# Row norms begun in the stage ahead of them, and half of a gather added by VectorE

## The chip, the cores and the metric

The kernel runs on one NeuronCore of a Trainium2 chip. The metric is the device time of one execution in microseconds (us), the median of the runs. TensorE (PE) multiplies and transposes into PSUM; VectorE (DVE), ScalarE (ACT) and GpSimd (POOL) work on SBUF and PSUM; SyncE and GpSimd start DMA transfers. Each engine runs its own program in order and meets the others by semaphores.

## What is computed

A residual stream `x` of 2 x 1024 tokens with 256 features passes four layers. Each layer norms the rows, applies an attention (or what stands for one), adds, norms again, applies a feed-forward part, and adds:

```python
def _layernorm(x, axis=-1, eps=1e-05):
    m = jnp.mean(x, axis=axis, keepdims=True)
    v = jnp.var(x, axis=axis, keepdims=True)
    return (x - m) / jnp.sqrt(v + eps)
...
    x = x + jnp.tanh(g_xattn[0]) * _L0_xattn_ref(_layernorm(x), ctx_1024, ...)
    x = x + jnp.tanh(g_ffn[0]) * _L0_ffn_ref(_layernorm(x), ...)
    x = x + jnp.tanh(g_xattn[1]) * _L1_xattn_ref(_layernorm(x), ctx_1024, ...)
    x = x + jnp.tanh(g_ffn[1]) * _L1_ffn_ref(_layernorm(x), ...)
    x = x + jnp.tanh(g_xattn[2]) * _L2_xattn_ref(_layernorm(x), ctx_1024, ...)
    x = x + jnp.tanh(g_ffn[2]) * _L2_ffn_ref(_layernorm(x), ...)
    x = x + jnp.tanh(g_xattn[3]) * _L3_xattn_ref(_layernorm(x), ctx_1024, ctx_1024)
    x = x + jnp.tanh(g_ffn[3]) * _L3_ffn_ref(_layernorm(x), ...)
```

The `..._ref` parts that matter here: `_L0_ffn_ref` sends each token to one of eight experts; `_L1_xattn_ref` is a cross attention to 154 context tokens with a second layernorm of its own (gain and shift) and an output gate; `_L1_ffn_ref` sends each token to 4 of 16 experts, with two shared ones; `_L2_xattn_ref` is a linear attention; `_L2_ffn_ref` is two layers of local attention (window 128), each with a feed-forward part; `_L3_xattn_ref` multiplies by the context with a gelu between, and `_L3_ffn_ref` is a feed-forward part with weights and activations quantised to 4 bits.

## The kernel before

The 2048 tokens are T = 16 tiles of 128 rows, in G = 4 groups of four tiles (GT = 4, GN = 512 tokens). `x_tok`, the stream with tokens on partitions, stays in SBUF throughout. Each stage is a block of per-engine programs, run in the order in which they are written; all engines meet at a barrier between blocks. PSUM is used as eight banks of 128 x 512 values.

A row norm is a block of its own, `layer_norm` (L107). What can be had of it earlier is already had in the stage before: `RowStats.take` (L93) makes the statistics of each row (BN_STATS L96, BN_AGGR L99, by tile) as soon as its last add is done. `layer_norm` then has one chain: variance plus epsilon on VectorE (L144, or L142 where a second norm follows the first at once, `again`), the square root on ScalarE (L174), the inverse and minus mean times inverse on VectorE (L147, L149), then the 16 tiles, 13 on VectorE (L152) and three on ScalarE (L170), into `xn`. TensorE transposes each tile twice (L163) into eight banks of four, and ScalarE copies each bank to `xT`, features on partitions (L189, or L191 with gain and shift). With `keep` the tiles stay as they are and nothing is transposed (before the local attention, where eight tiles are ScalarE's). `root_table` (L104) loads ScalarE's table for the square root at the end of the stage before.

The square root and the activations of the feed-forward parts need different tables, so going from one to the other takes an ACT_TABLE_LOAD.

`feed_forward` (L214) serves the routed part and the local ones. For each group of 512 tokens it goes through units `u`: TensorE makes the hidden products, ScalarE the activation (L356 in the routed part), VectorE the gated product `hidden` (L429, L440), TensorE the output product; weights are split in two parts (upper and rest) beside that, on ScalarE (`weights_upper`, L341) and GpSimd. At the end of a group VectorE adds to x (`take`, L399 to L403) and takes statistics. The place where one group ends and the next begins is called a boundary below.

The stage ahead of the cross attention (L1716 to L1773) returns the expert outputs to their tokens: 16 indirect DMAs started by GpSimd (L1720), each 128 rows of 256 values, added in flight to `x_tok`; beside it VectorE makes remainders of weights (L211), copies the context's values out of PSUM (L1736) with their tails (L1741), and takes the statistics of each group when its four transfers have landed. GpSimd then makes the remainder of `wq` and `gated_bias` (L1725). Earlier, in the expert stage, L680 scatters 16 such tiles without an add. The name `oT` stands for attention outputs with features on partitions, `sd`, `rstd` and `minus_mean_rstd` for the root, its inverse and minus mean times it, one column for a tile.

## Time and profile before

| | |
|---|---|
| median of 3 runs | 2498.22 us (2495.98 to 2506.04) |
| the profiled execution | 2497.99 us, its span 2495.7 us |
| TensorE (matmul) busy | 2052.7 us, 82% |
| VectorE busy | 1759.9 us, 71% |
| ScalarE busy | 1327.8 us, 53% |
| GpSimd busy | 1045.6 us, 42% |
| mean granted clock | 0.905 |

All times in the rows below are microseconds from the start of the span, unless a column says ns. In a row of the timeline the first number is the start, the second the length (of a whole run of equal instructions where `x13` stands at the end), then engine, line, operation, output and inputs; the square brackets hold the idle time of the engine ahead of it and what ended that. PEclk is the granted clock of TensorE as a share of full speed: 1.00 is its upper level, 2.4 GHz.

### The profile page before, as it was taken

Reading aid. Unit: us, or ns where it says so; the run is one execution under the profiler, and the core shown is the slowest. Engines: PE = TensorE matmul, PEld = TensorE weight load, DVE = VectorE, ACT = ScalarE, POOL = GpSimd, SP = SyncE. Lnnn points to the kernel's source line nnn. Section 1 sums busy time; section 2 is a strip of 40 time slices with the busy share of each in tenths; the row PEclk is TensorE's granted clock in tenths of the full one; section 3 lists DMA queues with packets and bytes.
Section 4 is the critical chain, followed back from the end, with each engine's and each line's share of the span. In section 5 each row is a group of like instructions: output and inputs, shape, how many; then the busy total and the mean of one; then the engine's idle time right before and its main releaser. Section 6 shows DMA issues by size and latency. Waiting matters only on the chain. (4 is left out here: it accounts for less than half of the span.)

```text
span 2495.7 us, 41249 instructions
## 1 busy us (share of the span) xinstructions
PE 2052.7 (82%) x14744; PEld 1486.0 (60%) x14744; DVE 1759.9 (71%) x3778; ACT 1327.8 (53%) x3064; POOL 1045.6 (42%) x1053
## 2 busy tenths in 40 slices
PE   6899999966589997799997879886998886985254
PEld 5444444456556665688886668675877775764122
DVE  6899999855655554776765676766666675668896
ACT  4488888834354443333332247473436564323797
POOL 1333233115543431455553654543535452422554
PEclk9899999988799998899998989998998988987586
DMA  4244344154300001100002000002000001000000
GB/s 110 33 55 50 48 54 54 23 217 126 57 1 1 1 1 81 51 1 1 1 1 87 1 1 2 1 2 95 1 1 1 1 1 38 1 35 25 0 1 34
DMA packets 29257, 80.81 MB, mean 32 GB/s; under 512 B 6016, under 2 KB 20096, under 8 KB 27392
## 3 DMA queue, kind: packets, MB, share of 16 engines
q0 software_dynamic: 11136, 22.38, 7.2%
q1 hardware_dynamic: 17920, 55.80, 6.5%
q8 instruction: 120, 1.97, 0.3%
q14 instruction: 81, 0.66, 0.1%
...
## 5 line engine op out<-in xcount | busy, mean ns | idle before, releaser
L3028 ACT ACTIVATE probs<-psum 128x512 f32<-128x512 f32 (+1 forms) x640 | 344.0, 601 | 91.7 <-PE psum L2952 76.4
L3070 DVE TENSOR_REDUCE max_parts<-psum 128x1 f32<-128x512 f32 x512 | 320.1, 685 | 26.3 <-PE psum L2890 20.5
L199 PE MATMUL psum<-x_upper,weights_upper 128*128 128x512 f32 (+2 forms) x556 | 220.8, 397 | 27.5 <-POOL weights_rest L211 12.9
L211 POOL TENSOR_TENSOR weights_rest<-L1f,weights_upper 128x256 fp32r<-128x256 f32 x216 | 179.6, 858 | 147.9 <-ACT weights_upper L341 147.9
L2952 PE MATMUL psum<-q_stack,k_stack 50*128 50x512 f32 (+1 forms) x640 | 235.4, 453 | 0.2 <-ACT probs L3028 0.2
L199 PE MATMUL psum<-x_rest,weights_upper 128*128 128x512 f32 (+2 forms) x556 | 217.4, 391 | 0.0
L199 PE MATMUL psum<-x_upper,weights_rest 128*128 128x512 f32 (+2 forms) x556 | 216.3, 389 | 0.0
L2890 PE MATMUL psum<-k_stack,q_stack 48*128 48x512 f32 x512 | 192.6, 465 | 12.5 <-ACT probs L3028 7.8
L2962 PE MATMUL psum<-probs,v_tok 128*17 128x256 f32 x2560 | 194.7, 386 | 0.2 <-ACT probs L3028 0.2
L199 PE MATMUL psum<-weights_upper,hidden_upper 128*128 128x256 f32 (+1 forms) x572 | 178.2, 312 | 5.2 <-DVE hidden_rest L211 2.7
L2526 POOL TENSOR_TENSOR probs<-probs,row_sum 128x1024 f32<-128x1024 f32 x64 | 121.0, 1894 | 138.5 <-DVE row_sum L2545 138.5
L211 POOL TENSOR_TENSOR weights_rest<-L2f,weights_upper 128x256 fp32r<-128x256 f32 (+1 forms) x144 | 104.6, 755 | 163.1 <-ACT weights_upper L341 163.1
L199 PE MATMUL psum<-weights_upper,hidden_rest 128*128 128x256 f32 (+1 forms) x572 | 163.2, 285 | 0.0
L199 PE MATMUL psum<-weights_rest,hidden_upper 128*128 128x256 f32 (+1 forms) x572 | 163.0, 285 | 0.0
L2890 PEld LDWEIGHTS psum<-k_stack,q_stack 48*128 48x128 f32 x512 | 79.9, 189 | 124.2 <-DVE max_parts L3070 72.4
L2494 ACT ACTIVATE probs<-probs,row_least 128x256 f32<-128x256 f32 x256 | 126.9, 498 | 40.4 <-DVE row_least L2539 40.4
L2653 POOL DMA_DIRECT2D q_stack<-q_parts x56 | 30.5, 544 | 264.2 <-PE psum L2952 264.2
L199 PEld LDWEIGHTS psum<-x_upper,weights_upper 128*128 128x128 f32 (+1 forms) x556 | 105.9, 190 | 51.9 <-issue 24.4
L1934 ACT ACTIVATE L1x<-psum,row_least 128x154 f32<-128x154 f32 x256 | 95.4, 399 | 76.5 <-DVE row_least L1989 76.5
L1971 POOL TENSOR_TENSOR L1x<-L1x,row_sum 128x512 f32<-128x512 f32 x64 | 67.7, 1058 | 160.5 <-DVE row_sum L1994 160.2
L211 DVE TENSOR_TENSOR hidden_rest<-hidden,hidden_upper 128x512 fp32r<-128x512 f32 (+1 forms) x143 | 129.2, 903 | 4.9
L2391 POOL TENSOR_TENSOR cos_part<-cos_part,sin_part 128x1024 f32<-128x1024 f32 x32 | 76.5, 2389 | 116.0 <-DVE sin_part L2358 116.0
...
## 6 DMA issues: line engine op xcount, KB each, us to landing
...
```

The source lines that it names most:

```text
L199: ins = pe.matmul(out, lhsT(a).bitcast(F32R), rhs(b).bitcast(F32R), start=start and n == 0, stop=stop and n == len(PASSES) - 1, skip_group ...
L211: return engine.tensor_tensor(dst.bitcast(F32R), src, up_part, ALU.subtract)
L1934: ins = act.activation(ex[:, n % NE, h, :], net.ps[:, SLOT + 2 * s + e, a * SC:(a + 1) * SC], ACT.Exp, bias=mn[:, s, e, a:a + 1], scale=-1 ...
L1971: pool.tensor_tensor(main, ex[:, n % NE, :, 0:P], spread(sm[:, n % NE, :], P), ALU.mult)
L2391: pool.tensor_tensor(cp, cp, s_part[:, t % NSP].rearrange("p a n -> p (a n)"), ALU.add).then_inc(added, 1)
L2494: ins = act.activation(pb[:, n % NPB, h, :], pb[:, n % NPB, h, :], ACT.Exp, bias=mn[:, n % NPB, h:h + 1], scale=-1.0, accum_out=sm[:, n % ...
L2526: pool.tensor_tensor(pb[:, n % NPB], pb[:, n % NPB], spread(sm[:, n % NPB, :], 2 * P), ALU.mult)\
L2890: ins = pe.matmul(out, qs[s][r, a * P:(a + 1) * P].bitcast(F32R), ks[s][r, k * 512:(k + 1) * 512].bitcast(F32R), start=True, stop=True)
L2952: pe.matmul(net.ps[0:m, ST + n % NS, :], ks[s][r, k * P:k * P + m].bitcast(F32R), qs[s][r, :].bitcast(F32R), start=True, stop=True).then_i ...
L2962: ins = pe.matmul(net.ps[32 * j:32 * j + HD + 1, PVB, 0:256], vt[:, b, k, h, :], pb[:, n % NPB, j * 256:(j + 1) * 256], start=k == 0, stop ...
L3028: act.activation(pb[0:m, n % NPB, (1 - e) * 512:(2 - e) * 512], net.ps[0:m, ST + (2 * n + e) % NS, :], ACT.Exp, scale=HD ** -0.5)\
L3070: ins = v.tensor_reduce(mx3[:, u % 2, a + 4 * e, k:k + 1], src, AX.X, ALU.max)
```

## The change

Five of the eight norms are changed: those before the cross attention, the routed part, the linear attention, the local attention and layer 3.

A new class `NormAhead` holds the steps of `layer_norm` as separate calls: `spread` (variance plus epsilon), `root`, `invert` (the inverse, and minus mean times it), `vector` and `scalar` (the tiles). The preceding stage calls them for twelve of the sixteen tiles: after each group of four where the stage goes by groups (cross attention's norm, and those before the linear attention and layer 3, which follow a feed-forward part), or once for twelve. The tiles are written to a buffer `nT` (`norm_turned` in the rows), or to `y` where nothing is transposed first. `norm_end` takes the place of `layer_norm`: statistics and norm of the last four tiles, all 32 transposes, and the copies out of PSUM, seven banks by ScalarE and one by VectorE. The transposes go in place: the banks are copied back to `nT`, which takes the place of `xT`. Several buffers of other stages share its room.

In the feed-forward parts the root comes at `u == 2` of the next group, the inverse at `u == 2` of VectorE's program, and ScalarE's four tiles at `u == 3`. The order of ScalarE's program then has 12 more table loads (two at each of six boundaries).

In the stage with the gather the first eight transfers write plain rows to the upper half of `nT`, and VectorE adds them to `x_tok`, four tiles at a time (L1906 of the changed kernel); the last eight add in flight as before. The remainder of `wq` and `gated_bias` go from GpSimd to VectorE, the tails of the context's values from VectorE to ScalarE.

VectorE in the stage with the gather, from the first copies of the context's values on, before (`row_stats` and `mean_var` are the statistics, `values` and `tail_values` the context's):

```order
L1736 COPY values<-psum 128x512 x2
L211 TENSOR_TENSOR wo_rest<-L1x,wo_upper 128x2048
L96 BN_STATS row_stats<-x_tok 128x6 x4
L99 BN_AGGR mean_var<-row_stats 128x2 x4
L1741 COPY tail_values<-psum 32x2x64 x8
L96 BN_STATS row_stats<-x_tok 128x6 x4
L99 BN_AGGR mean_var<-row_stats 128x2 x4
L1736 COPY values<-psum 128x512 x2
L96 BN_STATS row_stats<-x_tok 128x6 x4
L99 BN_AGGR mean_var<-row_stats 128x2 x4
L1741 COPY tail_values<-psum 32x2x64 x8
L96 BN_STATS row_stats<-x_tok 128x6 x4
```

and now (`rows_var_eps`, `rows_sd`, `rows_rstd` are columns of four tiles):

```order
L1900 COPY values<-psum 128x512 x2
L1906 TENSOR_TENSOR x_tok<-x_tok,norm_turned 128x1024
L98 BN_STATS row_stats<-x_tok 128x6 x4
L101 BN_AGGR mean_var<-row_stats 128x2 x4
L209 TENSOR_SCALAR rows_var_eps<-mean_var 128x4
L340 TENSOR_TENSOR wo_rest<-L1x,wo_upper 128x2048
L224 RECIPROCAL rows_rstd<-rows_sd 128x4
L226 SCALAR_TENSOR_TENSOR rows_minus_mean_rstd<-mean_var,rows_rstd 128x4
L1900 COPY values<-psum 128x512 x2
L340 TENSOR_TENSOR wq_rest<-L1x,wq_upper 128x2048
L1939 TENSOR_SCALAR gated_bias<-L1x,cross_factor 128x256
L1906 TENSOR_TENSOR x_tok<-x_tok,norm_turned 128x1024
```

The tails are gone, an add of 1024 elements precedes the statistics of a group, and the remainder of `wq` and the bias stand between the first and second group; the inverse for a group waits here for ScalarE's root.

ScalarE where the cross attention ends and the routed part begins, before (`oT_upper` is the attention's output, `warm` a dummy that loads the table):

```order
L1941 CAST oT_upper<-psum 128x512 x4
L104 ACT_TABLE_LOAD
L104 ACTIVATE warm<-warm 128x1
L1776 UNCONDITIONAL_BRANCH
L167 UNCONDITIONAL_BRANCH
L174 ACTIVATE sd<-var_eps 128x16
L170 ACTIVATE xn<-x_tok,minus_mean_rstd,rstd 128x256 x3
L189 COPY xT<-psum 128x512 x8
```

and now:

```order
L106 ACT_TABLE_LOAD
L106 ACTIVATE warm<-warm 128x1
L2112 CAST oT_upper<-psum 128x512 x2
L218 ACTIVATE rows_sd<-rows_var_eps 128x12
L243 ACTIVATE norm_turned<-x_tok,rows_minus_mean_rstd,rows_rstd 128x2x128 x8
L1947 UNCONDITIONAL_BRANCH
L299 UNCONDITIONAL_BRANCH
L305 COPY norm_turned<-psum 128x512 x2
L218 ACTIVATE rows_sd<-rows_var_eps 128x4
L305 COPY norm_turned<-psum 128x512
L243 ACTIVATE norm_turned<-x_tok,rows_minus_mean_rstd,rows_rstd 128x2x128
L305 COPY norm_turned<-psum 128x512 x4
```

The root for twelve tiles, and eight of those tiles, now precede the end of the stage (the first UNCONDITIONAL_BRANCH), and the root of the last four stands among the copies of the transposed banks.

ScalarE at a boundary of the routed part, before (`activated` is the gate's activation, `weights_upper` the upper parts of the weights of a unit):

```order
L341 CAST weights_upper<-L1f 128x256 x3
L356 ACTIVATE activated<-psum 128x512
L341 CAST weights_upper<-L1f 128x256 x3
L356 ACTIVATE activated<-psum 128x512
L341 CAST weights_upper<-L1f 128x256 x3
```

and now:

```order
L471 CAST weights_upper<-L1f 128x256 x3
L218 ACT_TABLE_LOAD
L218 ACTIVATE rows_sd<-rows_var_eps 128x4
L486 ACT_TABLE_LOAD
L486 ACTIVATE activated<-psum 128x512
L471 CAST weights_upper<-L1f 128x256 x3
L243 ACTIVATE norm_turned<-x_tok,rows_minus_mean_rstd,rows_rstd 128x2x128 x4
L486 ACTIVATE activated<-psum 128x512
```

The root with a table load on either side stands ahead of one activation, and the four tiles ahead of the next.

The diff, cut:

```diff
+class NormAhead:
+
+
+    def __init__(self, net, ctx, src, place, again=False):
+        self.net, self.src, self.place, self.again = net, src, place, again
...
+    def spread(self, v, lo, hi):
+
+        r = self.net.rows
+        if self.again:
+            ins = v.tensor_scalar(r.ve[:, lo:hi], r.mv[:, lo:hi, 1], 1.0 + EPS, EPS * EPS, ALU.mult, ALU.add)
+        else:
+            ins = v.tensor_scalar(r.ve[:, lo:hi], r.mv[:, lo:hi, 1], EPS, None, ALU.add)
+        ins.then_inc(self.var_ready, 1)
+
+    def root(self, act, part, lo, hi):
+
+        r = self.net.rows
+        act.wait_ge(self.var_ready, part + 1)
+        act.activation(r.sd[:, lo:hi], r.ve[:, lo:hi], ACT.Sqrt).then_inc(self.sd_ready, 1)
+
+    def invert(self, v, part, lo, hi):
+
+        r = self.net.rows
+        v.wait_ge(self.sd_ready, part + 1)
+        v.reciprocal(r.rs[:, lo:hi], r.sd[:, lo:hi]).then_inc(self.rs_ready, 1)
+        v.wait_ge(self.rs_ready, part + 1)
+        v.scalar_tensor_tensor(r.nb[:, lo:hi], r.mv[:, lo:hi, 0], -1.0, r.rs[:, lo:hi], ALU.mult, ALU.mult)\
+            .then_inc(self.rows_ready, 1)
+
+    def vector(self, v, tiles):
+
+        r = self.net.rows
+        for t in tiles:
+            dst, own = self.place(t)
+            v.tensor_scalar(dst, own(self.src), r.mv[:, t, 0:1], r.rs[:, t:t + 1], ALU.subtract, ALU.mult)\
+                .then_inc(self.normed, 1)
+
+    def scalar(self, act, part, tiles):
+
+        r = self.net.rows
+        act.wait_ge(self.rows_ready, part + 1)
+        for t in tiles:
+            dst, own = self.place(t)
+            act.activation(dst, own(self.src), ACT.Identity, bias=r.nb[:, t:t + 1], scale=r.rs[:, t:t + 1])\
+                .then_inc(self.normed, 1)
+
...
+def norm_end(net, ahead, parts, turns=None, xT=None, gain=None, shift=None, after=None):
+
+    nc = net.nc
+    LO = T - GT
...
+            step = Steps(v, vec)
+            net.rows.take(v, step, ahead.src, range(LO, T))
+            step.settle()
+            ahead.spread(v, LO, T)
+            ahead.invert(v, parts, LO, T)
+            ahead.vector(v, OWN)
+            if turns:
+                if after is not None:
+                    v.wait_ge(after.landed, 16)
+                v.wait_ge(early, BY_VECTOR + 1)
+                c = BY_VECTOR % C
+                if gain is None:
+                    v.tensor_copy(out(BY_VECTOR), net.ps[:, BY_VECTOR, :])
+                else:
+                    v.tensor_scalar(out(BY_VECTOR), net.ps[:, BY_VECTOR, :], gain[:, c:c + 1], shift[:, c:c + 1],
+                                    ALU.mult, ALU.add)
+
...
+            def _(pe):
+                for n in range(G * C):
+                    g, c = divmod(n, C)
+                    if n == BY_VECTOR:
+                        pe.wait_ge(ahead.normed, T)
+                    for t in range(g * GT, (g + 1) * GT):
+                        ins = pe.transpose(net.ps[:, n, t % GT * P:(t % GT + 1) * P], turns(t, c), net.ident[:])
+                    ins.then_inc(early, 1)
...
+                take(0)
+                take(1)
+            ahead.root(act, parts, LO, T)
+            if turns:
+                take(2)
+            ahead.scalar(act, parts, OTHER)
+            if turns:
+                for n in range(3, G * C):
+                    if n != BY_VECTOR:
+                        take(n)
...
+                if ahead is not None and g >= 1 and u == 2:
+                    ahead.root(act, g - 1, (g - 1) * GT, g * GT)
+                if ahead is not None and g >= 1 and u == 3:
+                    ahead.scalar(act, g - 1, range((g - 1) * GT, g * GT))
...
+                if ahead is not None and g == G - 1:
+                    return
                 net.rows.take(v, step, y if then is None else x, range(g * GT, (g + 1) * GT))
+                if ahead is not None:
+                    step.settle()
+                    ahead.spread(v, g * GT, (g + 1) * GT)
...
+                if ahead is not None and g >= 1 and u == 2:
+                    ahead.invert(v, g - 1, (g - 1) * GT, g * GT)
...
+            ahead.root(act, 0, 0, T - GT)
+            ahead.scalar(act, 0, range(GT, T - GT))
...
+            ahead.spread(v, 0, T - GT)
+            ahead.invert(v, 0, 0, T - GT)
+            ahead.vector(v, range(GT))
             for k in (PAIRS - 2, PAIRS - 1):
                 add_y(k)
-                statistics(k)
...
+        beside_x = lambda t, n: nT[:, t // GT, 2 * GN + t % GT * D:2 * GN + (t % GT + n) * D]
...
+                def tail_value(n):
+                    b, tail, half = v_items[n]
+                    act.wait_ge(v_made, n + 1)
+                    src = net.ps[:, 4 + n % 4, :]
+                    for i in range(4):
+                        r = slice(SEG * i, SEG * i + SEG)
+                        mine = lambda ap: ap.rearrange("p (q i) d -> p i q d", i=4)[:, i]
+                        ins = act.copy(mine(vz[r, b, half * 8:half * 8 + 8, :]),
+                                       mine(src[r].rearrange("p (h d) -> p h d", d=64)))
+                    ins.then_inc(tail_taken, 1)
...
+                act.wait_ge(cleared, 1)
+                tail_value(2)
+                tail_value(3)
+                for g in range(G - 1):
+                    ahead.root(act, g, g * GT, (g + 1) * GT)
+                    if g == 0:
+                        tail_value(6)
+                        tail_value(7)
+                    ahead.scalar(act, g, range(g * GT, (g + 1) * GT))
...
-                    pool.indirect_dma_start(x[:, t, :], None, slots_y, bass.IndirectOffsetOnAxis(slots[:, n:n + 1], 0),
-                                            compute_op=ALU.add)\
-                        .then_inc(gathered[t // GT], 16)
-                pool.wait_ge(wq_upper, 1)
-                rest(pool, wq[1][:], w("wq"), wq[0][:])
-                pool.tensor_scalar(gbo[:], w("bo"), factor, None, ALU.mult)
+                    at = bass.IndirectOffsetOnAxis(slots[:, n:n + 1], 0)
+                    if t < 2 * GT:
+                        pool.indirect_dma_start(beside_x(t, 1), None, slots_y, at).then_inc(gathered[t // GT], 16)
+                    else:
+                        pool.indirect_dma_start(x[:, t, :], None, slots_y, at, compute_op=ALU.add)\
+                            .then_inc(gathered[t // GT], 16)
...
+
+                def rows_of(g):
                     v.wait_ge(gathered[g], 16 * GT)
+                    if g < 2:
+                        xs = x[:, g * GT:(g + 1) * GT, :].rearrange("p t d -> p (t d)")
+                        step(v.tensor_tensor(xs, xs, beside_x(g * GT, GT), ALU.add))
+                        step.settle()
                     net.rows.take(v, step, x, range(g * GT, (g + 1) * GT))
+                    step.settle()
+                    ahead.spread(v, g * GT, (g + 1) * GT)
...
-                for n in range(len(v_items)):
-                    value(n)
-                    if n == 1:
-                        v.wait_ge(wo_upper, 1)
-                        rest(v, wo[1][:], w("wo"), wo[0][:])
-                    if n % 2:
-                        add(n // 2)
-
-        layer_norm(net, x, xT, again=True, gain=w("gain"), shift=w("shift"))
+                value(0)
+                value(1)
+                rows_of(0)
+                v.wait_ge(wo_upper, 1)
+                rest(v, wo[1][:], w("wo"), wo[0][:])
+                ahead.invert(v, 0, 0, GT)
+                value(4)
+                value(5)
+                v.wait_ge(wq_upper, 1)
+                rest(v, wq[1][:], w("wq"), wq[0][:])
+                v.tensor_scalar(gbo[:], w("bo"), factor, None, ALU.mult)
+                rows_of(1)
+                ahead.invert(v, 1, GT, 2 * GT)
+                rows_of(2)
+                ahead.invert(v, 2, 2 * GT, 3 * GT)
+                v.wait_ge(gathered[G - 1], 16 * GT)
...
+        norm_end(net, ahead, G - 1, lambda t, c: nT[:, c, t * P:(t + 1) * P], nT, gain=w("gain"), shift=w("shift"))
...
-                net.rows.root_table(act)
+                then.root(act, 0, 0, T - GT)
+                then.scalar(act, 0, range(GT, T - GT))
...
+                        if u == U + 1 and d == 0:
+                            then.invert(v, 0, 0, T - GT)
+                            then.vector(v, range(GT))
...
+                        if u == U and d == 1:
+                            step.settle()
+                            then.spread(v, 0, T - GT)
...
-                for k in range(6, 8):
-                    rows_of(k)
...
-            layer_norm(net, x, xT)
+            norm_end(net, routed, 1, turns, nT)
...
+                    norm_end(net, linear_in, G - 1, turns, nT)
...
+                norm_end(net, local_in, 1)
...
-                layer_norm(net, x, None, keep=y)
...
+                norm_end(net, last_in, G - 1, lambda t, c: y[:, t, c * P:(c + 1) * P], nT)
```

## Rows read from the trace of the kernel before

**Rows 1.** The cores: span and mean granted TensorE clock.
```profile
core 0: 2495.7 us, clock 0.905
```

**Rows 2.** Timeline, cross attention to routed layer: start, duration, engine, line, operation, idle.
```profile
981.94 0.75 DVE L2023 SCALAR_TENSOR_TENSOR x_tok<-psum,cross_factor,x_tok 128x512 f32<-128x512 f32 x1 [5.01 <-PE psum L1625]
984.30 0.25 DVE L99 BATCH_NORM_AGGREGATE mean_var<-row_stats 128x2 f32<-128x6 f32 x2
987.26 0.17 DVE L144 TENSOR_SCALAR var_eps<-mean_var 128x16 f32<-128x16 f32 x1 [2.71 <-PEq L3247]
988.10 4.28 DVE L152 TENSOR_SCALAR xn<-x_tok,mean_var,rstd 128x256 f32<-128x256 f32 x13
989.53 5.92 PE L163 MATMUL psum<-const,xn 128*128 128x128 f32 x32 [7.63 <-DVE xn L152]
990.68 0.58 ACT L189 COPY xT<-psum 128x512 f32<-128x512 f32 x1 [0.88 <-PE psum L163]
...
996.48 1.92 PE L477 MATMUL psum<-xT,const 128*32 128x512 f32 x16 [1.02 <-PEq L114]
```

**Rows 3.** Timeline, the norms before the linear attention and before layer 3.
```profile
1343.16 0.18 DVE L144 TENSOR_SCALAR var_eps<-mean_var 128x16 f32<-128x16 f32 x1 [3.04 <-PEq L3360]
1349.14 2.55 ACT L189 COPY xT<-psum 128x512 f32<-128x512 f32 x5 [0.27 <-PE psum L163]
...
2240.93 0.17 DVE L144 TENSOR_SCALAR var_eps<-mean_var 128x16 f32<-128x16 f32 x1 [2.86 <-PEq L3412]
2246.90 2.54 ACT L189 COPY xT<-psum 128x512 f32<-128x512 f32 x5 [0.27 <-PE psum L163]
```

**Rows 4.** Timeline of the gather and its norm; instructions of two lines (ns min/median/max).
```profile
657.52 2.28 DVE L211 TENSOR_TENSOR wo_rest<-L1x,wo_upper 128x2048 fp32r<-128x2048 f32 x1
...
676.48 1.41 DVE L96 BATCH_NORM_STATS2 row_stats<-x_tok 128x6 f32<-128x256 f32 x4 [3.36 <-DMA x_tok<-slots_y,slots]
678.10 1.52 POOL L1725 TENSOR_SCALAR gated_bias<-L1x,cross_factor 128x256 f32<-128x256 f32 x1
681.27 0.17 DVE L142 TENSOR_SCALAR var_eps<-mean_var 128x16 f32<-128x16 f32 x1 [2.98 <-PEq L1647]
684.70 5.93 ACT L191 ACTIVATE xT<-psum,L1x 128x512 f32<-128x512 f32 x8 [0.88 <-PE psum L163]
...
L680 POOL DMA_INDIRECT slots_x<-xn,slots x16: 965/969/1105, 552.5 to 571.7; - x16
...
L1720 POOL DMA_INDIRECT x_tok<-slots_y,slots x16: 1537/1546/3564, 642.2 to 672.6; - x16
```

**Rows 5.** Timeline, a group boundary of the routed layer; a table load.
```profile
1107.47 0.60 ACT L356 ACTIVATE activated<-psum 128x512 f32<-128x512 f32 x1 [1.95 <-PE psum L293]
1109.21 0.47 PE L199 MATMUL psum<-x_upper,weights_upper 128*128 128x512 f32 x1 [0.34 <-DVE hidden L440]
1112.46 0.60 ACT L356 ACTIVATE activated<-psum 128x512 f32<-128x512 f32 x1 [2.54 <-PE psum L293]
...
1333.17 1.28 ACT L104 ACT_TABLE_LOAD   x1
```

**Rows 6.** Second local feed-forward; windows: length, PE, PEld, DVE, ACT, POOL, PEclk.
```profile
2158.41 0.47 PE L199 MATMUL psum<-x_upper,weights_upper 128*128 128x512 f32 x1 [1.61 <-DVE hidden L429]
...
2150.00:2179.80 29.80, 28.19 (x156) 22.88 (x154) 18.71 (x34) 9.98 (x24) 12.37 (x18) 1.00 0.00 1
2179.80:2211.30 31.50, 30.52 (x153) 24.73 (x153) 18.37 (x34) 9.98 (x24) 13.01 (x18) 0.89 0.00 1
```

**Rows 7.** Timeline, the end of the linear attention and the norm behind it.
```profile
1428.76 0.59 ACT L1058 COPY oT<-psum 128x512 f32<-128x512 f32 x1 [2.91 <-PE psum L983]
1434.99 0.17 DVE L144 TENSOR_SCALAR var_eps<-mean_var 128x16 f32<-128x16 f32 x1 [1.74 <-PEq L81]
1435.94 4.04 ACT L170 ACTIVATE y_tok<-x_tok,minus_mean_rstd,rstd 128x256 f32<-128x256 f32 x8 [0.53 <-DVE minus_mean_rstd L149]
1440.29 3.64 PE L2261 MATMUL psum<-const,y_tok 128*128 128x128 f32 x16 [8.90 <-PEq L114]
```

141 lines of the change are left out of this document (87 added, 54 removed).

## The prediction, made before the change was run

> **What bounds the kernel now.** I began with spans and clock: one core, 2495.7 us [rows 1]; the profiled execution took 2497.99 us, 0.2 below the median of the runs (2498.22), so a sum made on the trace stands for the median within a microsecond. The stages run one after another and no single engine bounds all of them, so I read next the timeline where one stage ends and the next begins (a seam). There TensorE, busy on both sides, waits for a row norm. At the seam into the routed layer the last add into x starts at 981.94 and lasts 0.75, statistics follow until 984.55, the norm's first instruction comes at 987.26, TensorE transposes from 989.53 on (5.92 for 32), and the next stage's first matmul is at 996.48 [rows 2]: 13.8 us from the end of the add. The reader is to see that there the norm itself is the chain: VectorE, TensorE and ScalarE follow each other by tile. The seams before the linear attention and before layer 3 have the same form, 8.53 us (1343.16 to 1351.69) and 8.51 us (2240.93 to 2249.44) [rows 3]. Before the cross attention the timeline shows GpSimd as the latest: the gather, then two operations until 679.62, then a norm from 681.27 to 690.63 [rows 4].
>
> **The piece that all four seams share (`norm_end`).** Twelve of sixteen tiles are now normalised ahead, so TensorE may transpose at once. Three chains run in it. TensorE: 32 transposes, 5.92 [rows 2], then the copy of the last bank, 0.58 and 0.2 of latency: 6.7. VectorE: statistics of the last four tiles 1.9 (984.55 less 982.69), the chain of four short steps 0.84 (987.26 to 988.10), three tiles at 0.33 (4.28 over 13): 3.7 [rows 2], and the last eight transposes wait for it, which TensorE doesn't reach before 4.4 (24 of 32 of 5.92). ScalarE: first copy 1.15 after TensorE starts [rows 2], seven at 0.51 (2.55 over 5) [rows 3], a square root 0.2 and a tile 0.5: 5.5. TensorE is last, 6.6 to 6.7; I take 6.6. For the cross attention with gain and shift a copy takes 0.74 (5.93 over 8) [rows 4], so ScalarE is last: 1.15 + 5.2 + 0.7 = 7.1.
>
> **Part by part.** *Routed layer.* Add to norm was 4.57 with 1.86 of statistics in it; now 2.71. Then 6.6 and 0.3 to the next stage against 9.22 (987.26 to 996.48) [rows 2]. Saved: 13.8 - 9.6 = 4.2. The root, the inverse and the other twelve tiles lie under the 11 us in which TensorE makes the last output projection; if that cover were gone ScalarE's eight tiles alone would cost 4.0 [rows 7]. *Linear attention.* 8.53 + 1.86 - 6.6 = 3.8. *Layer 3.* The same with 8.51: 3.8. Their weights are fetched 1.9 earlier as well, so no landing becomes late.
>
> *Local attention.* Here nothing turns, and the gain vanishes into a new wait. VectorE now stands at `invert` until ScalarE has copied the last oT (1428.76 + 0.59) and taken the root: 1429.6. Behind it on VectorE are four tiles (1.4) and the last two adds into x, which end near 1432.9. ScalarE has eight tiles, 4.04 [rows 7], from 1430.1 to 1434.2, and ends the stage. Then 0.3 to `norm_end`, 1.9 + 0.8 + 1.1 in it and 1.75 for the barrier: 1440.1 against 1440.29 [rows 7]. The barrier's 1.75 is the idle time before 1434.99. Saved: 0.2, between -0.8 and 1.0.
>
> *The stage with the gather.* Before, the last transfer lands and statistics start at 676.48; GpSimd ends at 679.62 and the norm starts at 681.27 [rows 4]. The remainder of wq and the bias leave GpSimd, so its tail goes. What is late next is a chain through VectorE and ScalarE. From 657.5 VectorE has: add 1.15 (half of the 2.28 for 2048 elements), statistics and variance 2.2, wo 2.28, inverse 0.5, two value copies 1.3, wq 2.28, bias 0.4, add and statistics 3.3, root and inverse 0.8, statistics 2.2: 673.9. Then root, inverse 0.8 and ScalarE's four tiles 2.1: 676.8, +0.3 for the barrier: 677.1. The tail values moved to ScalarE lie before this: it had nothing to do from the end of its table load to the norm.
> The transfers must also be there. One issue with add in flight takes 1.55, with up to 3.56 beside VectorE's wo remainder; the plain scatter takes 0.97 [rows 4]. The trace has no plain gather, so its issue lies between 0.97 and 1.55. I take 0.97, as the scatter is the same instruction without the add. Eight issues less 0.58 are 4.6 saved; the added VectorE work may hold issues up by some 1.6 (wo held one up by 2.0). The last landing goes from 676.4 to 673.5, before 676.8, and is hidden. With 1.55 it would be 678.1. Dearer than 1.55 I exclude, the same 128 rows without the add; below nothing there is no price. Saved: 690.63 - (677.1 + 7.1) = 6.4; 4.9 with the dear issue.
>
> *Added inside the stages.* Two feed-forwards (routed, second local) get, at three group boundaries each, on VectorE a settle and a variance (0.3) and an inverse (0.5), on ScalarE two table loads of 1.28, a root 0.2 and four tiles 2.1. The first sits straight ahead of the product that TensorE waits for at the boundary (0.34 in the routed layer [rows 5], 1.61 in the local one [rows 6]): 0.3 each, 1.8 in all. The inverse comes where VectorE has caught up: nothing. ScalarE: its activations at the boundary start at 1107.47 and 1112.46, 4.99 apart, with 1.6 of its own work between [rows 5]; root and loads (2.8) fit into the 3.4 left, the tiles (2.1) into the next. If that cover were gone, see below. The cross attention pays 0.3 for the same variance ahead of its last remainder.
>
> **Sum.** 6.4 + 4.2 + 3.8 + 3.8 + 0.2 = 18.4 saved, 2.1 paid: 16.3. From 2498.2 that is 2481.9; I say 2482.
>
> **Rivals.** *The gather stays the bound* (plain issue 1.55, VectorE's new operations delay issues). For: 3.56 in place of 1.55 beside one VectorE operation. Against: the scatter's 0.97. Then that seam saves 4.9 or, with 2 us more of delay, 3: total 13 to 15, 2484.
> *The clock falls at more boundaries.* The second local feed-forward's group 2179.80 to 2211.30 had a clock of 0.89, and TensorE was busy for 30.52 in it against 28.19 for the same work in the group before (1.00) [rows 6], each after a pause of about 1.6. If longer pauses do this at all six boundaries, five new ones cost 2.0 each: 6 saved, 2492. Against: two of three such pauses did nothing to it.
> *ScalarE's table changes are dearer.* In the trace the load lasts 1.28, and nothing stands between it and the operations about it [rows 5]. If each change cost 1.4 more, boundaries would have 5.5 in 3.4 of room, 2.1 late at six places: 3.7 saved, 2494.5. The Trainium skill ("ScalarE: Activation LUTs", What ACT_TABLE_LOAD costs) says just this, a load of about 1283 ns and a drain of about 1380 ns, 2.66 us for every change. The load agrees with the trace, the drain isn't seen there.
> *Slower.* ScalarE is in order: if the three activations behind each root have no room, the 4.9 us of loads, root and tiles and the 0.8 on VectorE reach TensorE at six places, 34 us against 18.4: 2514. It decides once a boundary costs more than 3.1 us. Against: TensorE has two more units' products in hand before it needs an activation, and ScalarE idles 1.95 and 2.54 before them [rows 5].
> *It doesn't shorten the seams* (transposes at a low clock and the copies make `norm_end` as long as the old norm less its statistics): 4 x 1.9 + 4 saved, less 2: 2489.
>
> **How the numbers follow.** Forecast 0.58; gather 0.15; clock 0.13; tables 0.03; seams not shorter 0.07; slower 0.04. A measurement of this kernel tells about 0.5% (12.5 us) from no change, so faster means below 2485.7: the forecast and most of the gather's rival, 0.73; within 0.5%: 0.23; slower 0.04. The forecast's own spread (norm_end 5.8 at a full clock or 7.3, boundaries 0 to 0.8 each, gather seam 4.9 to 7) is 2476 to 2486. To leave no more than 0.2 out, the range reaches to the clock's case: 2475 to 2492.
>
> **What would show it.** Transposes start with the block, and `norm_end` lasts 6.6 (7.1 in the cross attention); the stage with the gather ends with ScalarE's tiles, not with GpSimd; plain gathers take 0.97 to issue; TensorE waits 0.6 and 1.9 at the boundaries; the next stage starts at the local attention as before. Wrong would be: a ScalarE activation that TensorE waits for right behind a root, a plain gather as dear as the adding one, low clock in more groups, or a wait for weights behind a shorter norm.

## The result and the profile after

The changed kernel took 2479.31 us (median of four runs, 2475.72 to 2483.35), 0.992 of before (95% interval 0.9903 to 0.9938), 19.5 us less than the 2498.80 of the four runs of before that stood beside it. It was measured again beside the experiments, six runs each: 2474.77 (ratio 0.9905, 0.9881 to 0.9929) and 2473.85 (0.9893, 0.9877 to 0.9908). Over the 16 runs the median is 2475.2; over 41 runs of before it is 2499.0. The forecast was 2482 with a range of 2475 to 2492.

The profiled execution is the slowest of the first four (2483.35), so its span is only 14.3 us shorter than that of [rows 1]:

```profile
core 0: 2481.4 us, clock 0.909
```

I cut both executions at the same points of the program. Each line below is one window of the changed kernel: its length, the busy time of PE, PEld, DVE, ACT and POOL with counts, the granted clock, the DMA share and GB/s. The windows are, in order:

- up to the first product of the keys;
- from there to the first query product (the stage with the gather and its norm);
- from the end of the cross attention's last add to the routed part's first product;
- three groups of the routed part, from add to add;
- from its last add to the linear attention's first product;
- the linear attention, up to the first product of the local one;
- from the second local feed-forward's first add to layer 3's first product.

```profile
0.00:650.10 650.10, 563.50 (x4976) 300.86 (x4977) 516.77 (x1005) 437.08 (x877) 186.19 (x290) 0.93 0.41 76
650.10:691.89 41.79, 26.09 (x128) 22.66 (x128) 29.92 (x70) 28.47 (x63) 23.41 (x16) 0.82 0.26 47
981.42:989.85 8.43, 3.90 (x32) 3.49 (x33) 3.96 (x16) 4.39 (x10) 0.04 (x1) 1.00 0.82 321
1096.05:1329.09 233.04, 231.31 (x1318) 195.43 (x1316) 162.90 (x254) 97.89 (x225) 127.03 (x150) 1.00 0.00 1
1329.09:1340.49 11.40, 5.36 (x32) 5.18 (x33) 5.36 (x17) 4.43 (x10) 0.04 (x1) 0.85 0.66 255
1340.49:1428.52 88.03, 70.99 (x304) 52.68 (x305) 55.88 (x132) 27.60 (x47) 52.43 (x42) 0.89 0.07 29
2142.61:2242.02 99.41, 84.62 (x464) 69.61 (x465) 63.00 (x128) 47.32 (x97) 31.91 (x45) 0.95 0.10 38
```

The lengths beside those of before and of the two later profiles of the same kernel, in us:

| stretch | before | after | again | again_2 |
|---|---|---|---|---|
| first key to first query product | 48.65 | 41.79 | 42.30 | 42.28 |
| cross attention's last add to routed part | 13.79 | 8.43 | 8.43 | 9.98 |
| three groups of the routed part | 232.35 | 233.04 | 232.99 | 233.00 |
| last routed add to linear attention | 15.51 | 11.40 | 11.42 | 11.40 |
| linear attention to local attention | 87.93 | 88.03 | 88.04 | 88.04 |
| first add of the second local part to layer 3 | 102.92 | 99.41 | 99.44 | 100.85 |
| sum of these, against before | | -19.05 | -18.53 | -15.60 |
| all the rest of the span, against before | | +4.75 | -5.47 | +10.60 |

The reader is to see two things. The stretches that the change touches agree from profile to profile, and give 15.6 to 19 us. The rest does not agree: it moves by 16 us between profiles of one kernel. Up to the first key product the code is the same as before, and it took 644.60 us before and 650.10, 643.58 and 654.90 after.

One part of this rest lies right behind a touched stretch, and the prediction has no term for it. These are the first 12 us of the local attention, before, in the changed kernel and in its third profile (again_2):

```profile
1440.29:1452.29 12.00, 10.51 (x46) 8.98 (x47) 5.65 (x11) 4.18 (x7) 0.00 (x0) 0.82 0.00 0
1428.52:1440.52 12.00, 10.51 (x34) 8.65 (x35) 3.17 (x7) 3.37 (x5) 0.00 (x0) 0.53 0.00 1
1438.66:1450.66 12.00, 10.50 (x41) 8.83 (x41) 4.32 (x8) 4.17 (x7) 0.00 (x0) 0.67 0.00 1
```

The granted clock was 0.82 before and 0.53 and 0.67 in these two; in the same 10.5 us TensorE has 46 matmuls before, 34 and 41 after. From the first product to ScalarE's eighth `squares` of that stage it took 42.70 us before, and 45.34, 45.34 and 44.04 in the three profiles of the changed kernel, so 1.3 to 2.6 us are lost there. Other kernels with the same norm ahead of it took 42.69 to 45.37, so these runs don't show that the shorter norm is the cause.

At the seam into the routed part, against [rows 2], transposes start with the block, beside the statistics, and the old chain VectorE, TensorE, ScalarE is gone:

```profile
980.67 0.75 DVE L2197 SCALAR_TENSOR_TENSOR x_tok<-psum,cross_factor,x_tok 128x512 f32<-128x512 f32 x1 [5.01 <-PE psum L1769]
984.14 2.81 PE L296 MATMUL psum<-const,norm_turned 128*128 128x128 f32 x24 [3.52 <-PEq L3423]
984.81 1.07 ACT L305 COPY norm_turned<-psum 128x512 f32<-128x512 f32 x2 [11.64 <-PE psum L296]
...
986.73 1.05 DVE L234 TENSOR_SCALAR norm_turned<-x_tok,mean_var,rows_rstd 128x256 f32<-128x256 f32 x3
987.84 1.09 PE L296 MATMUL psum<-const,norm_turned 128*128 128x128 f32 x8 [0.89 <-DVE norm_turned L234]
...
989.85 1.92 PE L618 MATMUL psum<-norm_turned,const 128*32 128x512 f32 x16 [0.92 <-PEq L263]
```

The short norm, up to the next stage's first product, takes 5.7 us (984.14 to 989.85), and 8.43 pass from the end of the add (980.67 + 0.75) to the next stage, where it was 13.8.

The stage with the gather, against [rows 4]:

```profile
673.29 0.34 DVE L1939 TENSOR_SCALAR gated_bias<-L1x,cross_factor 128x256 f32<-128x256 f32 x1
675.09 1.53 POOL L1890 DMA_INDIRECT x_tok<-slots_y,slots  x1 [0.30 <-issue]
680.12 2.07 ACT L243 ACTIVATE norm_turned<-x_tok,rows_minus_mean_rstd,rows_rstd 128x256 f32<-128x256 f32 x4 [0.44 <-DVE rows_minus_mean_rstd L226]
682.50 1.41 DVE L98 BATCH_NORM_STATS2 row_stats<-x_tok 128x6 f32<-128x256 f32 x4 [2.41 <-PEq L1792]
...
686.50 2.77 ACT L307 ACTIVATE norm_turned<-psum,L1x 128x512 f32<-128x512 f32 x4
...
L1888 POOL DMA_INDIRECT norm_turned<-slots_y,slots x8: 949/956/1957, 647.7 to 658.4; - x8
...
L1890 POOL DMA_INDIRECT x_tok<-slots_y,slots x8: 1531/1546/3643, 659.6 to 675.1; - x8
```

GpSimd ends at 676.6 and ScalarE's last tiles end the stage at 682.2, 32.1 us behind the first key product; the forecast had 32.5 (677.1 less 644.6). A plain transfer takes 0.95 us to issue, one that adds 1.55. The long ones have a neighbour on VectorE:

```profile
667.05 2.28 DVE L340 TENSOR_TENSOR wo_rest<-L1x,wo_upper 128x2048 fp32r<-128x2048 f32 x1
667.10 3.64 POOL L1890 DMA_INDIRECT x_tok<-slots_y,slots  x1 [0.30 <-issue]
671.05 1.53 POOL L1890 DMA_INDIRECT x_tok<-slots_y,slots  x1 [0.30 <-issue]
671.08 2.30 DVE L340 TENSOR_TENSOR wq_rest<-L1x,wq_upper 128x2048 fp32r<-128x2048 f32 x1
```

The issue that began 0.05 us behind the start of a remainder took 3.64; the one that began 0.03 ahead of the next remainder took 1.53, though the two ran side by side.

A boundary of the routed part, against [rows 5], and the one of the second local part, against [rows 6]:

```profile
1099.03 0.60 ACT L486 ACTIVATE activated<-psum 128x512 f32<-128x512 f32 x1 [1.95 <-PE psum L423]
1100.98 0.47 PE L328 MATMUL psum<-x_upper,weights_upper 128*128 128x512 f32 x1 [0.57 <-DVE hidden L579]
1101.49 1.28 ACT L218 ACT_TABLE_LOAD   x1
1102.79 0.21 ACT L218 ACTIVATE rows_sd<-rows_var_eps 128x4 f32<-128x4 f32 x1
1103.01 1.28 ACT L486 ACT_TABLE_LOAD   x1
1104.30 0.60 ACT L486 ACTIVATE activated<-psum 128x512 f32<-128x512 f32 x1
1106.61 2.08 ACT L243 ACTIVATE norm_turned<-x_tok,rows_minus_mean_rstd,rows_rstd 128x256 f32<-128x256 f32 x4
1108.66 0.60 ACT L486 ACTIVATE activated<-psum 128x512 f32<-128x512 f32 x1
...
2150.91 0.47 PE L328 MATMUL psum<-x_upper,weights_upper 128*128 128x512 f32 x1 [1.83 <-DVE hidden L568]
```

TensorE waits 0.57 and 1.83 us. The activation behind the root starts at 1104.30, 5.27 after the one before; their regular distance is 4.4 (1104.30 to 1108.66), so it is 0.9 late. TensorE has no second wait behind it.

### The profile page after: what moved, and what is told of

It reads as the page before. It is cut to its first block and busy times, and to the rows that moved or that the text cites. A ratio compares the mean times of both kernels' runs of the same rounds, so it can differ in the third digit from the quotient of the medians.

```text
span 2481.4 us, 41330 instructions
## 1 busy us (share of the span) xinstructions
PE 2054.0 (83%) x14744; PEld 1484.2 (60%) x14744; DVE 1747.8 (70%) x3765; ACT 1364.9 (55%) x3137; POOL 1038.5 (42%) x1051
```

## The experiments

Each starts from the changed kernel. Lengths of stretches come from one profile of each. I trust these over the whole times, since the whole also carries what the unchanged stages do. Four kernels have one run each, so their whole times prove little: 2490.52 us with more table changes, 2487.41 with late transposes, 2479.79 with the remainder of wq on GpSimd and 2491.36 with only the norm ahead.

### All transfers add in flight

```diff
-                    if t < 2 * GT:
+                    if t < 0:
                         pool.indirect_dma_start(beside_x(t, 1), None, slots_y, at)...
-                    if g < 2:
+                    if g < 0:
                         xs = x[:, g * GT:(g + 1) * GT, :].rearrange("p t d -> p (t d)")
```

> The changed kernel, but all sixteen transfers of the gather add in flight and VectorE adds nothing. My theory: the plain rows give GpSimd 0.6 us for each of eight transfers and cost VectorE 1.22 for each of two adds. In the profile of the changed kernel the stage ends with ScalarE's tiles (682.2), 0.4 us behind them the last transfer could land; with all in flight GpSimd ends some 4 us later and so is the last of the stage, while VectorE and ScalarE are 2.4 earlier. Expected: the stage (first key product to the first query product) takes 43 to 45 us in place of 41.8, that is 1 to 3 us more, and the whole 1 to 3 us more than the changed kernel. Rival 'the plain rows are what the gather stage gained': the stage goes back by 4 us or more, towards 48.7. Rival 'the plain rows bring nothing': it stays within 0.5 us or gets faster by the 2.4 of the adds.

Measured: first key to first query product 43.04 us, so the plain rows are worth 1.25 us against the first profile of the changed kernel and 0.75 against the other two. The last issue starts 28.5 us behind the first key product (25.0 in the changed kernel), and the stage now ends with it:

```profile
678.88 2.07 ACT L243 ACTIVATE norm_turned<-x_tok,rows_minus_mean_rstd,rows_rstd 128x256 f32<-128x256 f32 x4 [0.44 <-DVE rows_minus_mean_rstd L226]
679.78 1.55 POOL L1890 DMA_INDIRECT x_tok<-slots_y,slots  x1 [0.30 <-issue]
...
684.56 1.41 DVE L98 BATCH_NORM_STATS2 row_stats<-x_tok 128x6 f32<-128x256 f32 x4 [5.71 <-PEq L1792]
```

ScalarE's tiles end at 680.95, the last transfer has been issued at 681.33 and lands after that. The stage went as expected. The whole did not: 2492.84 us (six runs, 2486.46 to 2493.97), 13.5 more than the changed kernel's first result. I ran it again beside the changed kernel on one chip.

> The kernel with all sixteen transfers adding in flight once more, beside the changed kernel on one chip. On the first chip it took 2492.8 us, where its stage is only 1.25 us longer than the changed kernel's (43.04 against 41.79). Theory 'the 11 us beyond are the clock of that chip': here it takes 0 to 4 us more than the changed kernel. Rival 'transfers that add in flight slow later stages': it again takes 8 us or more beyond the changed kernel.

Measured: 2479.78 (ratio to before 0.9931, 0.991 to 0.9952) beside 2473.85 for the changed kernel; the stage took 43.10 us. So of the 12 us that the first run took beyond its stage some 5 are left. Both theories miss: I had given 0 to 4 for the one and 8 or more for the other. The unchanged part of its first profile was 13.5 us longer than before, of its second 2.5 us shorter. What makes it so stays open.

### The remainder of wq on GpSimd again

```diff
             def _(pool):
...
+                pool.wait_ge(wq_upper, 1)
+                rest(pool, wq[1][:], w("wq"), wq[0][:])
+                pool.tensor_scalar(gbo[:], w("bo"), factor, None, ALU.mult)
```

(and the same lines taken out of VectorE's program)

> The changed kernel with one move undone: the remainder of wq and the gated bias are GpSimd's again, behind its last transfer. My theory: the gather stage got shorter because its last chain ran through GpSimd (3.9 us for the two behind the last transfer in the trace before), not only because its transfers are cheaper. In the changed kernel GpSimd ends its last transfer at 676.6; with the two operations it ends near 680.5 to 682.5 (the add on VectorE holds it up), and VectorE is 2.6 us earlier, so ScalarE's tiles end near 679.6. Expected: the stage takes 41 to 43 us in place of 41.8, near to nothing either way, since the plain transfers have made room for them; together with the all-in-flight run this would say that either edit alone is enough and that the second adds little. Rival 'the move is what counted': the stage goes back by 3 us or more.

Measured: 45.00 us, 3.2 more than in the changed kernel's first profile and 2.7 more than in the one on the same chip (42.30). My expectation was wrong, and what came is the rival's 3 us, or a little less. The rows:

```profile
675.70 5.26 DVE L226 SCALAR_TENSOR_TENSOR rows_minus_mean_rstd<-mean_var,rows_rstd 128x4 f32<-128x4 f32 x1
675.86 5.08 POOL L340 TENSOR_TENSOR wq_rest<-L1x,wq_upper 128x2048 fp32r<-128x2048 f32 x1
...
680.88 1.39 DVE L98 BATCH_NORM_STATS2 row_stats<-x_tok 128x6 f32<-128x256 f32 x4
...
681.00 2.07 ACT L243 ACTIVATE norm_turned<-x_tok,rows_minus_mean_rstd,rows_rstd 128x256 f32<-128x256 f32 x4 [5.54 <-DVE rows_minus_mean_rstd L226]
...
683.60 2.07 ACT L243 ACTIVATE norm_turned<-x_tok,rows_minus_mean_rstd,rows_rstd 128x256 f32<-128x256 f32 x4 [0.44 <-DVE rows_minus_mean_rstd L226]
```

An operation on four columns, 0.16 us elsewhere in the same stage, took 5.26 us: it ended when GpSimd's operation of 5.08 us ended, and statistics and ScalarE's tiles stood behind it. GpSimd itself was done at 681.84; the stage ends with ScalarE's tiles at 685.67. I had reckoned the engines' work apart; here one holds up the other. The Trainium skill ("SBUF — State Buffer", Who interferes with whom) says that VectorE and GpSimd share a pair of SBUF ports and that the one that holds it blocks the other for its whole instruction; the 5.26 beside 5.08 agrees, though by the rows VectorE's operation began 0.16 us ahead of GpSimd's. In the same section the Trainium skill infers that a two-input VectorE operation doesn't hold up GpSimd's making of descriptors. The issue of an indirect transfer is held up all the same: an adding transfer took 3.56 us beside the 2048-element remainder, and 3.64 in the changed kernel, in place of 1.55. Both began while the remainder ran, and both ended 1.4 us behind its end. An indirect transfer also takes its row numbers from `slots`, a tile in SBUF, so these rows don't tell whether that read is held up or the descriptors are.

### Only the norm ahead

Both edits of the gather taken back together.

```diff
-                    if t < 2 * GT:
+                    if t < 0:
...
+                rest(pool, wq[1][:], w("wq"), wq[0][:])
```

> The changed kernel with both edits of the gather taken back: all transfers add in flight, and the remainder of wq and the gated bias are GpSimd's behind the last of them; the norm ahead stays. My theory: GpSimd is the last again, 30.0 + 5.1 + 0.9 us behind the first key product, as before the change (35.0), and only the shorter norm is left as a gain, 9.4 less 6.8 us. Expected: the stretch from first key product to first query product takes 46 to 47.5 us (48.65 before, 43.0 without the plain rows, 45.0 without the move). Rival 'the edits are worth the same alone and together': 41.8 + 1.25 + 3.2 = 46.2; rival 'the norm ahead gives the whole': below 44.

Measured: 46.50 us. In this stage the norm ahead saves 2.15 us (48.65 less 46.50). From there the plain rows bring 1.5 (to 45.00) or the move 3.4 (to 43.07, the mean of 43.04 and 43.10). Both bring 4.2 to 4.7, so the two edits nearly add up. They don't meet in one queue, though. Here GpSimd is the last of the stage: its `gated_bias` ends at 680.66 and the statistics behind the stage's end start at 682.31. With all transfers adding it is a transfer's landing, and with the remainder on GpSimd it is ScalarE, which waited for VectorE, which waited for GpSimd.

### The tail shared

```diff
-                    ahead.scalar(act, g, range(g * GT, (g + 1) * GT))
+                    ahead.scalar(act, g, range(g * GT, (g + 1) * GT - (2 if g == 2 else 0)))
+                    if g == 0:
+                        act.activation(gbo[:], w("bo"), ACT.Identity, scale=factor)
...
                 ahead.invert(v, 2, 2 * GT, 3 * GT)
+                ahead.vector(v, (3 * GT - 2, 3 * GT - 1))
```

> The changed kernel with its last chain in the gather stage shortened: the gated bias is ScalarE's (between its first and second group of tiles, where it waited 2.3 us), and of the third group's four tiles VectorE does two beside ScalarE's two. My theory: that stage now ends with VectorE's work and ScalarE's last four tiles (680.12 to 682.19); 0.34 us of VectorE's work and 1.0 of ScalarE's go. Expected: the stretch from first key to first query product takes 40.3 to 40.9 us in place of 41.8 (42.3 in its second profile). Rival 'a transfer is the last by then': it stays within 0.3 us.

Measured: 41.06 us, 0.7 to 1.2 less than the changed kernel's three profiles, a little short of what I expected. That the stage ends with VectorE and ScalarE is so. The whole took 2481.49 us (0.9917, 0.9896 to 0.9939), so a gain of the whole can't be shown: it drowns in what the unchanged stages do.

### The feed-forward parts without the norm ahead

```diff
-                         ahead=linear_in)
+                         ahead=None)
...
-                    norm_end(net, linear_in, G - 1, turns, nT)
+                    layer_norm(net, x, nT, keep=y)
```

(and the same for `last_in`)

> The changed kernel with the old row norm before the linear attention and before layer 3 (nothing of it in the two feed-forward parts ahead). My theory: these two seams give 4.1 and 3.5 us back and the six boundaries save about 0.25 us each, so 7.6 - 1.5 = 6 us more than the changed kernel; the wait of TensorE at a boundary goes back from 0.57 to 0.34 and from 1.83 to 1.6 us, and groups of the routed part from 79.69 to 79.44 us. Rival 'boundaries cost nothing by themselves, the difference of the two profiles is chance': groups stay at 79.7. Rival 'the seams gain only what the clock gives': each seam gives back under 2 us.

Measured: the two seams 15.65 and 19.89 us (11.40 and 16.29 in the changed kernel, 15.51 and 19.78 before), the three routed groups 232.36 (233.04, 232.35). Everything is back to within 0.2 us of before, and all else of the change stays. The touched stretches are 11.6 us shorter than before, and the whole is 11.5 shorter: 2487.51 beside 2498.99 (0.9955, 0.9941 to 0.9968). So on the medians the account by stretches closes here, though this kernel's own profile was, with 2496.90, among its slower runs and 10.8 us longer in the unchanged rest. A boundary costs 0.23 us (233.04 less 232.36, over three).

### More table changes at the boundaries

```diff
...
                     ahead.root(act, g - 1, (g - 1) * GT, g * GT)
+                    for _ in range(g - 1):
+                        for f in (func, ACT.Sqrt):
+                            net.spare = getattr(net, 'spare', 1) + 1
+                            act.activation(net.rows.warm[:, net.spare:net.spare + 1], net.rows.warm[:, 0:1], f)
```

> The changed kernel with more table changes of ScalarE at the boundaries of the routed and of the second local feed-forward part: none more at the first boundary, one pair (activation's table and back, 2 x 1.28 us and two dummies of 0.2, 3.0 us) behind the root at the second, two pairs (6.0 us) at the third. My theory: in the changed kernel the activation behind the root is 0.9 us later than its turn in the routed part and nobody waits for it, since TensorE has two units in hand; a unit of TensorE takes 4.4 us there. The first boundary stays at 79.7 us for its group; with 3.0 us more the activation is 3.9 late, within one unit, and TensorE waits under 1 us; with 6.0 us more it is 6.9 late and TensorE waits 1.5 to 4 us. In the local part the second boundary costs under 1 us and the third 1 to 4. Rival 'no room was left' (the price of the slower case): the second boundary already costs 3 us and the third 6. Rival 'ScalarE has room for all': neither moves by 0.3 us.

Measured: routed groups 79.68, 79.68 and 78.02 us (79.69, 79.64 and 73.71 in the changed kernel). So 3.0 us more of loads cost nothing, and 6.0 us cost 4.3. The new wait of TensorE at the third boundary:

```profile
1266.90 0.47 PE L328 MATMUL psum<-x_upper,weights_upper 128*128 128x512 f32 x1 [0.56 <-DVE hidden L583]
...
1278.42 0.47 PE L328 MATMUL psum<-x_upper,weights_upper 128*128 128x512 f32 x1 [2.49 <-DVE hidden L583]
```

The second of these rows is the 2.49 us that TensorE newly waits for a product whose activation was late. The other 1.8 us are the clock behind that wait. In the routed groups of the changed kernel it was 1.00 throughout; here, from the end of the wait on:

```profile
1278.42:1290.00 11.58, 11.57 (x55) 9.47 (x56) 9.21 (x13) 5.81 (x15) 7.46 (x9) 0.85 0.01 1
```

At 0.85 for 11.58 us about 1.7 are lost (my estimate, 0.15 of the window). In the local part the second boundary is unchanged and the third costs 1.9 (25.58 against 23.73). So the mechanism of the prediction's slower case exists, but ScalarE can be at least 3.0 us later than the change makes it before TensorE waits. The 3.1 us in that case are another quantity, what each boundary would have to cost TensorE to eat up the gain.

### Late transposes at one seam

```diff
-                    if n == BY_VECTOR:
+                    if n == (0 if late else BY_VECTOR):
                         pe.wait_ge(ahead.normed, T)
```

(ScalarE's root and tile ahead of its first copies, for this seam alone)

> The changed kernel with one seam altered, from cross attention to the routed part: TensorE begins its transposes only when all sixteen tiles are normed, and ScalarE takes the root and its tile before its first copy. TensorE's pause goes from 3.5 to about 7 us, as long as before the change (7.6). Two causes are told apart for the 1.2 us that this seam gained beyond the forecast, and the 1.8 us that the first group behind it gained. Theory 'clock': with the short pause the granted clock stayed at 1.00 through the seam (24 transposes in 2.81 us, 0.117 each) where it was 0.63 before; with the long pause it falls, 32 transposes take 5.5 to 6 us, and the first group of the routed part goes back from 106.2 to 107 or 108 us. The seam is then 3.4 + 2 to 3 longer. Rival 'the order': the transposes keep 0.117 each, only the wait is added (3.4 us), and the first group stays at 106.2.

Measured: the seam 13.75 us, before's 13.79, with the norm's twelve tiles still ahead. TensorE's pause is 7.21 us and its 32 transposes took 6.42:

```profile
985.36 6.42 PE L296 MATMUL psum<-const,norm_turned 128*128 128x128 f32 x32 [7.21 <-DVE norm_turned L234]
```

The three kernels beside it had a seam of 9.0, with a pause of 3.51 and transposes of 5.35, so 3.7 of the added 4.8 us are the wait and 1.1 the clock. What the seam gains is that TensorE works beside VectorE's statistics, not that tiles are made elsewhere: without that overlap nothing is left. (The old norm had an overlap of its own, transposes beside the making of tiles, which this kernel lacks as well.) That fits the prediction's account of three chains. On the clock this run looked like a proof. The first group behind the seam took 108.33 us, as 'clock' wanted. But all three kernels beside it took 108.33 to 108.35 with the short pause, so that part had nothing to do with the edit.

### TensorE kept busy

```diff
+def keep_busy(net, pe, bank, n):
+    for _ in range(n):
+        pe.transpose(net.ps[:, bank, 0:P], net.ident[:], net.ident[:])
...
+            if ahead is not None:
+                keep_busy(net, pe, GATE, 12)
```

(20 more in the short norm ahead of the local attention, 24 in the stage with the gather)

> The changed kernel with transposes of the identity added on TensorE where it only waits; their results are read by nobody: 12 at the end of the two feed-forward parts that precede a norm, 20 in the short norm before the local attention, and 24 in the stage of the gather, from the point where the second group's row columns are ready. My theory: after a shorter pause the granted clock is higher, and a part of the time at the seams is TensorE at the lower level (32 transposes took 5.36 us at a mean clock of 0.74 before the linear attention and 2.81 for 24 where the clock had stayed at 1.00; the first 10 us of the local attention had 0.50). Expected: the transposes before the linear attention and layer 3 take 3.9 to 4.7 us, the seams get 0.3 to 1 us shorter each (ScalarE's copies are next, 5.5), the local attention begins at a higher clock and gains 1 to 3 us; sum 2 to 5 us less than the changed kernel. Rival 'the clock after a pause does not hang on these pauses' (or the added work itself draws the clock down): no stretch changes by 0.3 us, or other stretches give it back.

Measured: 2475.89 us (0.9899, 0.9882 to 0.9915) beside 2474.77, no gain. At the seam before the linear attention the pause ahead of the transposes went from 4.80 to 3.49 us, and they took longer, 6.51 in place of 5.36:

```profile
1333.85 5.36 PE L296 MATMUL psum<-const,norm_turned 128*128 128x128 f32 x32 [4.80 <-PEq L3546]
```

and with the added transposes:

```profile
1335.32 6.51 PE L296 MATMUL psum<-const,norm_turned 128*128 128x128 f32 x32 [3.49 <-PEq L3560]
```

That seam became 1.1 us longer (12.56 against 11.42), and the linear attention behind it 1.5 (89.52 against 88.04 to the first local product). The local attention did get faster, 43.49 us to the eighth `squares` against 45.34, but other kernels of that chip without the added work had 44.00 and 42.73, so this gain is not shown either. 'The clock follows the pause' falls with this. At the seam into the routed part a pause of 3.5 us was followed by transposes of 3.90 us in five profiles, 5.35 in six and 6.34 in one. Four kernels of one chip had 3.90, and on another three of three had 5.35, which looked like a mark of the chip until the next run:

> The changed kernel on the chip of the three runs beside it. Two things are open. Its first and second measurement gave 19.5 and 23.9 us less than before, while the seven changed stretches of the profiles add up to 18.7; and on one chip the seam into the routed layer took 8.43 us in four kernels of four, on another 9.0 in three of three. Theory 'the rest is the clock of unchanged stages, and differs by chip': the seam takes 8.4 or 9.0 here in all kernels of this call alike, the changed stretches again add up to 18 to 19.5 us, and what the whole deviates from that goes with the mean granted clock. Rival 'a gain of the change that I have not found': the difference is 22 us or more at an equal sum of the stretches and with no difference in unchanged stages.

There the seam took 9.98 us in the changed kernel and 9.00, 8.99 and 8.99 in its three neighbours on the same chip. Neither theory of that run holds in full: the seam differs within one chip, and the difference to before was 27 us (2473.85 against 2500.82) where the stretches gave 15.6, though in a profile that was itself the slowest run of six (2492.64).

### The changed kernel again

> The changed kernel itself once more, on the chip of the runs beside it. In the runs so far, stages of unchanged code differ from profile to profile (the part up to the first key product took 644.6 us before and 646.3 to 654.9 since, the mean granted clock 0.90 to 0.91), and the changed kernel's first profile had a seam into the routed layer at clock 1.00 (8.43 us) where three others had 0.81 (9.0 us). Theory 'additive seams': changed places save 18.7 us together, so the time is 0.9915 to 0.9935 of before. Rival 'the first four runs were lucky with the clock': the ratio is 0.9945 or more, and the seam takes 9.0 us.

Measured: 0.9905, and a seam of 8.43 us. Neither number of the rival came; the theory's ratio (0.9915 to 0.9935) was missed too, on the fast side. The runs of this kernel go with the mean clock: 2467.08 us at 0.916, 2473.66 at 0.915, 2480.38 at 0.910, 2485.31 at 0.908. The profiles of this run and of again_2:

```profile
core 0: 2471.7 us, clock 0.915
...
core 0: 2490.7 us, clock 0.902
```

### The local attention's norm undone

```diff
-                norm_end(net, local_in, 1)
+                layer_norm(net, x, None, keep=y)
```

(with the calls of `ahead` taken out of the linear attention, and its last statistics back)

> The changed kernel with the norm before the local attention undone: the linear attention takes the statistics of all its tiles, nothing of the norm is ahead in it, and the old norm follows. My theory: that seam gained nothing (88.03 against 87.93 us from the first product of the linear attention to the first of the local one), because ScalarE's eight tiles moved into the stage and its end came later by as much as the norm got shorter. Expected: 87.7 to 88.2 us for that stretch, the whole within 0.2 us of the changed kernel in the profile's stretch. Rival 'the gain is there and hidden by chance': the stretch gets longer by 0.5 us or more.

Measured: 88.56 us from the linear to the local attention, 0.5 more than the changed kernel (88.04) and 0.6 more than before (87.93). That is just the rival's 0.5. The norm ahead gains half a microsecond there, and another thing of the change loses as much: the barrier that frees semaphores now stands behind this norm, not ahead of it. From the last add to the next product it is 8.73 us in this run against 8.11 before with the same norm. The whole, 2473.70, is the changed kernel's (2474.77 beside it). In this run the local attention took 42.73 us to the eighth `squares`, the changed kernel on the same chip 45.34: if that came from the norm, its half microsecond is more than paid for behind it. Kernels with the norm ahead that took 42.7 speak against it.

## Why the prediction was right

**The four seams.** The three chains in `norm_end` were costed from rows 2 and 3 at 6.6 us to the last copy. Measured to that copy it takes 5.97 before the linear attention (1333.85 to 1339.82), 5.85 before layer 3 and 5.41 at the routed part, where the clock was 1.00. The statistics that leave the way to the norm were counted at 1.86 us; from the last add to the norm's start it is only 1.55 less before the linear attention (4.76 against 6.31) and 0.8 less before layer 3 (4.65 against 5.46). The two errors offset each other, and that the savings of two seams come out so near is partly luck. Saved were to be 3.8 before the linear attention, measured 4.1; before layer 3 3.8, measured 3.5 (2.1 in again_2); at the routed part 4.2, measured 5.4, 4.8 or 3.8, as TensorE's clock was 1.00, 0.81 or 0.66 in it. I had sized the transposes at the low clock of [rows 2], which is one of the three.

**The stage with the gather.** Forecast 6.4, measured 6.9, 6.35 and 6.35. The chain through VectorE and ScalarE was right to 0.4 us, the plain issue (taken as 0.97 from the scatter, measured 0.95) and the norm with gain (7.1, measured 7.0: 682.50 to 689.53) too. What the working did not say is how the gain divides. I wrote that the tail on GpSimd goes; the move of wq and the bias was the largest part (2.7 to 3.4 us), the norm ahead is worth 2.15, and the plain rows, which I worked out at length, 0.8 to 1.5.

**The local attention.** Forecast 0.2, between -0.8 and 1.0; measured -0.1.

**What it pays.** Forecast 0.3 for each of six boundaries, 1.8 in all. TensorE's waits came as given (0.6 and 1.9, measured 0.57 and 1.83), so 0.23 each, 1.4 in all. The 0.3 in the cross attention can't be read: its stretch took 289.5 us before and 286.0 to 290.7 after. The 3.4 us of room on ScalarE were overrated by 0.9, which cost nothing, as the two units in TensorE's hand covered it.

**The rivals.** The gather as the bound: no, GpSimd has issued its last transfer 5.6 us ahead of the end of the stage; its mechanism is there, though, in the 3.64 us of one issue. The clock at more boundaries: no. The routed groups have 1.00 all through, and there it fell only in the kernel with more table changes, behind a wait of 2.49 us. In the second local part the slow group has moved from the third (31.50 us before, 29.68 now) to the fourth (22.16, 23.74) in all three profiles of the changed kernel, and there is still one. Dearer table changes: no, the load takes 1.28 us, and the next operation starts 0.01 to 0.02 behind it in the rows above. By the drain of 1.38 us that the Trainium skill ("ScalarE: Activation LUTs", What ACT_TABLE_LOAD costs) adds, the activation at a boundary would have been 2.8 us later (an estimate, two changes of 1.38); no row shows it. Seams not shorter: only where the overlap is undone.

**The sum.** Forecast 16.3. The touched stretches gave 15.6 to 19.05, the medians 19.5 to 27. The forecast is right for the stretches. The range held the first median (2479.31), and the two later ones (2474.77, 2473.85) lie just below its low end, so that the whole fell inside is partly luck. The step that did not hold is in the first sentence of the working, that a sum made on the trace stands for the median within a microsecond: that takes the unchanged 1995 us as fixed, and they moved by 16 us between profiles. Its low end, 2475, was made from the touched stretches alone. Half of the chance for 'within 0.5%' went to the clock rival, whose mechanism is real, but in stages that I never looked at (the start of the local attention is one) and in both directions. Whether the change raises the clock in unchanged stages (the mean was 0.908 to 0.916 in 15 of 16 runs, against 0.902 to 0.907 before) or the runs had it by chance, these runs can't tell. Part of a higher mean is arithmetic: if all 19 us had gone from time at the lower level, 0.905 would become 0.908 (my estimate from the span of before). What lies above that is open; the kernel with only the gather's adds undone had 0.903 to 0.910.
